# A recurrent scan on one core: 64-column tiles throughout, biases as weight rows, and both wrap pieces made on GpSimd

## The reference

```
x = x + conv3x3(gn(x)) + bias
x = x + scan(gn(x))
x = x + irfft2(low modes of rfft2(gn(x)), mixed over channels by w2)
x = x + irfft2(rfft2(gn(x)), mixed over channels by w3) + bias
```

```
x_  = [prev shifted down | prev | prev shifted up]       # along the rows, 96 features
i   = x_ @ weight_ih.T + bias_ih ;  h = cur @ weight_hh.T + bias_hh
r   = sigmoid(r_i + r_h) ; z = sigmoid(z_i + z_h) ; n = tanh(n_i + r * n_h)
new = n * z + cur * (1 - z)
```

## Time and profile before

| | |
|---|---|
| median of 3 runs | 661.55 us (659.97 to 664.05) |
| the profiled execution | 663.57 us, its span 661.8 us |
| PE busy | 595.9 us (90%) |
| DVE busy | 497.6 us (75%) |
| ACT busy | 456.2 us (69%) |
| POOL busy | 269.6 us (41%) |
| mean granted TensorE clock | 0.974 |
| the scan | about 132 to 377 us of the span |

### The profile page before, as it was taken

The page is one execution under the profiler, slowest core; times in us unless marked ns, Lnnn a source line. Parts: engine busy times, 40 slices in busy tenths (PEclk is TensorE's granted clock), DMA queues, the critical chain, the costliest instruction groups (busy, mean ns, idle before and its releaser), DMA issues.

```text
span 661.8 us, 19857 instructions
## 1 busy us (share of the span) xinstructions
PE 595.9 (90%) x6860; PEld 478.5 (72%) x6860; DVE 497.6 (75%) x1277; ACT 456.2 (69%) x932; POOL 269.6 (41%) x378
## 2 busy tenths in 40 slices
PE   4689888799999999999999999998878777799996
PEld 2223223478888888888888899997666666799996
DVE  6476685557777777777777768789889889867776
ACT  2345657877777777777777897776748997684442
POOL 6454546135555555554555430104485544202200
PEclk9799898979999999999999999999899998899999
DMA  6800000011111111111111210000316665203314
GB/s 236 316 1 0 1 0 9 0 31 35 36 34 34 35 36 34 34 36 34 35 34 36 62 79 1 1 1 1 129 34 219 201 212 164 96 1 128 128 78 176
DMA packets 31200, 45.63 MB, mean 69 GB/s; under 512 B 7088, under 2 KB 25520, under 8 KB 30272
## 3 DMA queue, kind: packets, MB, share of 16 engines
q1 hardware_dynamic: 30080, 44.98, 21.0%
q10 hardware_dynamic: 672, 0.15, 0.1%
q0 software_dynamic: 416, 0.07, 0.1%
HBM read 28.53 MB, written 8.39 MB: 56 GB/s over the span
## 4 chain that ended last, share of the span: by engine, by line
PE 71%; DVE 16%; issue 5%; ACT 5%; POOL 1%; DVEq 0%; ACTq 0%; POOLq 0%
PE psum L634 16%; PE psum L627 13%; PE psum L595 9%; PE psum L618 8%; DVE work L321 5%; PE psum L707 5%; PE psum L845 5%; PE psum L861 5%; PE psum L723 3%; PE psum L765 3%; ACT work L326 2%; DVE small L1161 2%; PE psum L834 2%; PE psum L691 2%; DVE spec L345 1%
## 5 line engine op out<-in xcount | busy, mean ns | idle before, releaser
L634 PE MATMUL psum<-spec,matrices 128*64 128x128 f32 x1512 | 111.7, 283 | 1.0 <-issue 1.0
L627 PE MATMUL psum<-spec,matrices 128*128 128x128 f32 x756 | 106.4, 277 | 2.3 <-DVE spec L1259 2.3
L486 POOL TENSOR_TENSOR spec<-spec 32x120 f32<-32x120 f32 x126 | 59.8, 474 | 119.0 <-DVE spec L1275 119.0
L595 PE MATMUL psum<-spec,matrices 128*64 128x512 f32 x384 | 94.2, 648 | 15.1 <-ACT spec L886 7.5
L765 PE MATMUL psum<-work 128*32 128x128 f32 x2368 | 77.4, 286 | 24.5 <-ACT work L326 22.2
L627 PEld LDWEIGHTS psum<-spec,matrices 128*128 128x128 f32 x756 | 95.2, 193 | 2.5 <-DVE spec L1259 2.5
L634 PEld LDWEIGHTS psum<-spec,matrices 128*64 128x64 f32 x1512 | 81.0, 138 | 16.5 <-issue 1.5
L765 PEld LDWEIGHTS psum<-work 128*32 128x32 f32 x2368 | 68.3, 115 | 33.4 <-issue 27.3
L595 PEld LDWEIGHTS psum<-spec,matrices 128*64 128x64 f32 x384 | 29.9, 148 | 72.8 <-issue 65.7
L321 DVE TENSOR_TENSOR work<-spec,psum 32x512 f32<-32x512 f32 x108 | 73.5, 680 | 9.1 <-PE psum L765 5.8
L461 POOL TENSOR_SCALAR spec<-image,small 32x960 f32<-32x960 f32 (+1 forms) x48 | 55.5, 1157 | 53.2 <-DVE small L1148 28.7
(11 more groups left out here) (140 smaller groups left out, 982.4 us busy)
## 6 DMA issues: line engine op xcount, KB each, us to landing
work<-w_dram SPq DMA_DIRECT2D x33, 512.0 KB, 3.4
spec<-work SPq DMA_DIRECT2D x252, 32.0 KB, 1.8
image<-x_dram SPq DMA_DIRECT2D x3, 2048.0 KB, 11.6
out_dram<-image SPq DMA_DIRECT2D x3, 2048.0 KB, 6.3
image<-x_dram SPq DMA_DIRECT2D x4, 512.0 KB, 5.9
work<-w_dram SPq DMA_DIRECT2D x1, 2048.0 KB, 7.6
out_dram<-image SPq DMA_DIRECT2D x4, 512.0 KB, 2.9
kept<-const_dram SPq DMA_DIRECT2D x1, 192.0 KB, 5.9
```

Source lines behind the costliest of these rows:

```text
L486: nc.gpsimd.tensor_tensor(lower_edge(h, parity), below(mix[h]), below(keep[h]), ALU.subtract).then_inc(lower_ready[h], 1)
L595: last_mm = mm(psum[o, n % 4, :], cv[:, kx, o], rows_[:, 8 * half:8 * half + 8, kx:kx + W], start=kx == 0, stop=kx == 2)
L627: mm(psum[:, 4 * h + g, 0:HB], sv[:, g, :], state[h], start=True, stop=False)
L634: last = mm(psum[o, 4 * h + g, 0:HB], sv[:, 3 + g, o], e, start=False, stop=True)
```

## The change

- **Tiles.** `from_state` issues two matmuls of 64 weight columns for each sum in place of one of 128. The h sum is no longer made by L618 from `columns` but by two 64-column matmuls from the edge buffers, whose current rows and ones it uses (weights of block 6). So all 14 matmuls of a half-step have 64 columns (6 from the state, 8 from the edges).
- **Order.** State part of r and n; wait for the edges; edges of r, of h, of n; state part of z; edges of z. VectorE waits for a new semaphore `h_sum`.
- **Biases.** VectorE spreads them in a zeroed 128 x 128 buffer `bias_z` (a memset and three small copies), TensorE turns them with eight small matmuls against the identity, and ScalarE writes them in two copies into the weight rows that the ones meet. This stands between the third and the fourth convolution group. ScalarE's activations have no bias any more, and pre1 is a plain product.
- **Wrap pieces.** GpSimd makes the lower one, waits for it, makes the upper one from `mix` and `keep`, waits for it, and then adds the state. ScalarE's copy is gone.
- **DMAs.** The edge buffers of the two halves lie side by side, so SP fetches a column for both halves in two DMAs of 256 columns, after z_sum of both halves. Only column 1 is fetched for each half apart.

```diff
         def edges_of(h, parity):
-            at_ = (2 * h + parity) * HB
+            at_ = (2 * parity + h) * HB
...
+            def current(w, parity):
+                for e, q in SIDES:
+                    sp.dma_start(e[q, parity * 2 * HB:(parity + 1) * 2 * HB],
+                                 columns[q, ds(w * (2 * HB), 2 * HB)]).then_inc(cur_in[parity], 16)
...
                     for h in range(2):
                         sp.wait_ge(z_sum[h], i * 2 + (k + 1))
-                        current(h, i * 2 + (k + 3), (k + 1) % 2)
+                    current(i * 2 + (k + 3), (k + 1) % 2)
...
                 nc.gpsimd.tensor_tensor(lower_edge(h, parity), below(mix[h]), below(keep[h]),
                                         ALU.subtract).then_inc(lower_ready[h], 1)
+                pool.wait_ge(lower_ready[h], w + 1)
+                nc.gpsimd.tensor_tensor(upper_edge(h, parity), above(mix[h]), above(keep[h]),
+                                        ALU.subtract).then_inc(sedge_ready[h], 1)
+                pool.wait_ge(sedge_ready[h], w + 1)
                 pool.wait_ge(state_ready[h], w + 1)
                 add_state(h, w)
...
+            pe.wait_ge(const_in, 32)
+            pe.wait_ge(bias_spread, 4)
+            for g in range(4):
+                for row in (C, 2 * C):
+                    last = mm(psum[row:row + C, 5, P * g:P * g + P], bias_z[:, C * g:C * g + C], cm["ident"],
+                              start=True, stop=True)
+            last.then_inc(bias_turned, 1)
             conv_group(NG - 1, False, True)
...
+            def from_state(h, w, g):
+                if g == 0:
+                    pe.wait_ge(state_ready[h], w)
+                for o in HALVES:
+                    mm(psum[o, 4 * h + g, 0:HB], sv[:, g, o], state[h], start=True, stop=False)
+
+            def from_edges(h, g, parity, starts=False):
+                for o, e in zip(HALVES, edges_of(h, parity)):
+                    last = mm(psum[o, 4 * h + g, 0:HB], sv[:, 3 + g, o], e, start=starts, stop=True)
+                return last
+
+            def half_step(h, w, parity, nth):
+                from_state(h, w, 0)
+                from_state(h, w, 2)
+                if nth is None:
+                    pe.wait_ge(cur_first[h], 32)
+                else:
+                    pe.wait_ge(cur_in[parity], nth * 32)
                 pe.wait_ge(sedge_ready[h], w)
                 pe.wait_ge(lower_ready[h], w)
+                from_edges(h, 0, parity).then_inc(r_sum[h], 1)
+                from_edges(h, 3, parity, True).then_inc(h_sum[h], 1)
+                from_edges(h, 2, parity).then_inc(n_sum[h], 1)
+                from_state(h, w, 1)
+                from_edges(h, 1, parity).then_inc(z_sum[h], 1)
...
+            for row, o in ((C, slice(P // 2, P)), (2 * C, slice(0, P // 2))):
+                a(sv[row:row + C, 3:7, o], turned[row:row + C, :, o], ACT.Copy).then_inc(bias_written, 1)
...
-            def state_edges(h, w, parity):
-                act.wait_ge(state_ready[h], w + 1)
-                s = state[h].rearrange("p (b h) -> p b h", h=H4)
-                up = edges_of(h, parity)[0].rearrange("p (b h) -> p b h", h=H4)
-                a(up[P - C:P, :, 1:H4], s[P - C:P, :, 0:H4 - 1], ACT.Copy).then_inc(sedge_ready[h], 1)
...
+            def scan_step(w):
+                for h in range(2):
+                    gates(h, w)
+                    candidate(h, w)
...
+            v.memset(bias_z, 0.0).then_inc(bias_spread, 1)
+            dve.wait_ge(bias_spread, 1)
+            v.tensor_copy(bias_z[:, 0:3 * C:C + 1], bias_s[:, 0:3]).then_inc(bias_spread, 1)
+            v.tensor_copy(bias_z[:, 3:3 + C + 2:C + 1], bias_s[:, 3:5]).then_inc(bias_spread, 1)
+            v.tensor_copy(bias_z[:, 3 * C + 5:3 * C + 6], bias_s[:, 5:6]).then_inc(bias_spread, 1)
...
             def new_state(h, w):
+                dve.wait_ge(h_sum[h], w)
                 dve.wait_ge(r_gate[h], w)
-                v.scalar_tensor_tensor(out=pre1[h], in0=psum[:, 4 * h + 3, 0:HB], scalar=bias_s[:, 5:6], in1=gr[h],
-                                       op0=ALU.add, op1=ALU.mult).then_inc(reset_done[h], 1)
+                v.tensor_tensor(pre1[h], gr[h], psum[:, 4 * h + 3, 0:HB], ALU.mult).then_inc(reset_done[h], 1)
```

More of the change, by code:

```diff
@@ L153, in edges_of @@
         def edges_of(h, parity):
-            at_ = (2 * h + parity) * HB
+            at_ = (2 * parity + h) * HB
             return upper_e[:, at_:at_ + HB], lower_e[:, at_:at_ + HB]
         gr, gz, gn, pre1, pre2, keep, mix = [[scan_buf() for _ in range(2)] for _ in range(7)]
+        bias_z = spec[:, off:off + 4 * C]
         columns = work[:, 0:B * ROWS]
@@ L198, in program @@
         columns_ready, last_columns = sem("columns_ready"), sem("last_columns")
-        bias_ready = sem("bias_ready")
-        cur_in = [[sem(f"cur_in{h}{parity}") for parity in range(2)] for h in range(2)]
+        bias_spread, bias_turned, bias_written = map(sem, ("bias_spread", "bias_turned", "bias_written"))
+        cur_first = [sem(f"cur_first{h}") for h in range(2)]
+        cur_in = [sem(f"cur_in{parity}") for parity in range(2)]
         state_ready = [sem(f"state_ready{h}") for h in range(2)]
         sedge_ready = [sem(f"sedge_ready{h}") for h in range(2)]
+        h_sum = [sem(f"h_sum{h}") for h in range(2)]
         lower_ready = [sem(f"lower_ready{h}") for h in range(2)]
@@ L386, in _, with first_current @@
             sp.dma_start(forward_m, const_d[:, sum(KEPT_COLS.values()):]).then_inc(const_in, 16)
[L388 to L392 removed]
+            SIDES = ((upper_e, slice(0, P // 2)), (lower_e, slice(P // 2, P)))
+            def first_current(h):
+                for e, q in SIDES:
+                    sp.dma_start(e[q, 2 * HB + h * HB:2 * HB + (h + 1) * HB],
+                                 columns[q, 2 * HB + h * HB:2 * HB + (h + 1) * HB]).then_inc(cur_first[h], 16)
+            def current(w, parity):
+                for e, q in SIDES:
+                    sp.dma_start(e[q, parity * 2 * HB:(parity + 1) * 2 * HB],
+                                 columns[q, ds(w * (2 * HB), 2 * HB)]).then_inc(cur_in[parity], 16)
             sp.wait_ge(pads_zeroed, 12)
             sp.wait_ge(columns_ready, B // 2)
[L396 to L397 removed]
+            first_current(0)
             sp.wait_ge(columns_ready, B)
             sp.wait_ge(last_columns, 1)
[L400 to L401 removed]
+            first_current(1)
+            current(2, 0)
             with sp.Fori(0, (W - 4) // 2) as i:
@@ L473, in lower_edge, with upper_edge, above @@
                 return edges_of(h, parity)[1].rearrange("p (b h) -> p b h", h=H4)[0:C, :, 0:H4 - 1]
+            def upper_edge(h, parity):
+                return edges_of(h, parity)[0].rearrange("p (b h) -> p b h", h=H4)[P - C:P, :, 1:H4]
+            def above(buf):
+                return buf.rearrange("p (b h) -> p b h", h=H4)[P - C:P, :, 0:H4 - 1]
             def below(buf):
@@ L493, in _ @@
                 nc.gpsimd.tensor_copy(lower_edge(h, 1), below(state[h])).then_inc(lower_ready[h], 1)
+                pool.wait_ge(lower_ready[h], 1)
+                nc.gpsimd.tensor_copy(upper_edge(h, 1), above(state[h])).then_inc(sedge_ready[h], 1)
+                pool.wait_ge(sedge_ready[h], 1)
                 add_state(h, 0)
@@ L613, in _ @@
             keep_warm(WARM_CONV_NORM, group_m)
-            def from_column(h, w):
-                mm(psum[:, 4 * h + 3, 0:HB], sv[:, 6, :], columns[:, ds(w * (2 * HB) + h * HB, HB)],
-                   start=True, stop=True)
-            def banks_free(h, w):
-                pe.wait_ge(reset_done[h], w - 1)
-            def from_state(h, w, parity, nth):
-                pe.wait_ge(state_ready[h], w)
-                for g in (0, 2, 1):
-                    mm(psum[:, 4 * h + g, 0:HB], sv[:, g, :], state[h], start=True, stop=False)
-                pe.wait_ge(cur_in[h][parity], nth * 32)
+            HALVES = [slice(i * (P // 2), (i + 1) * (P // 2)) for i in range(2)]
@@ L629, in from_state @@
                 pe.wait_ge(sedge_ready[h], w)
                 pe.wait_ge(lower_ready[h], w)
-                for g, s in ((0, r_sum), (2, n_sum), (1, z_sum)):
-                    for i, e in enumerate(edges_of(h, parity)):
-                        o = slice(i * (P // 2), (i + 1) * (P // 2))
-                        last = mm(psum[o, 4 * h + g, 0:HB], sv[:, 3 + g, o], e, start=False, stop=True)
-                    last.then_inc(s[h], 1)
+                from_edges(h, 0, parity).then_inc(r_sum[h], 1)
@@ L659, in _ @@
             with pe.Fori(0, (W - 4) // 4) as i:
                 for k in range(4):
-                    scan_step(i * 4 + (k + 2), k % 2, i * 2 + (1 + (k + 1) // 2))
-            scan_step(W - 2, 0, W // 2 - 1)
-            from_state(0, W - 1, 1, W // 2)
-            banks_free(1, W - 1)
-            from_column(1, W - 1)
-            from_state(1, W - 1, 1, W // 2)
+                    for h in range(2):
```

(6 more changed lines are left out.)

59 lines of the change are left out of this document (17 added, 42 removed).

## The result

The changed kernel takes 665.57 us (median; 663.60 to 667.22), the one before 662.72 us beside it on the same chip: a ratio of 1.0044 [1.0030, 1.0058], 2.9 us. The forecast was 672, slower by 1.6%. The profiled execution has a span of 664.1 us.

What follows compares the result with a forecast made beforehand. The prediction took TensorE at 1.89 us a half-step as the bound, the recurrence loop nearly as long. Its terms, 0 + 9.5 + 0.5 + 0 - 0.3 + 0.6 = +10.3 us on a median of 661.55, gave 672 us, range 657 to 689.

Steps and rivals of the forecast that it cites:

- likeliest case: Scan: half the mixes caught by GpSimd's add, half-step 1.92 to 2.05 us, 665 to 682 us; chance 0.46.
- border gain: TensorE in the scan: 0.35 us a half-step at two tile-width changes, 44 us by itself, but off the path.
- recurrence: Scan's loop through ScalarE, VectorE and GpSimd to TensorE: 3.78 us, 1.89 for a half-step, so 0 us.
- contention: VectorE's mix waiting for GpSimd's add in SBUF: half caught, mean 0.15 us a loop, +9.5 us, bounds 0 and +25.
- VectorE's loop border: VectorE idle 0.24 us once in six half-steps, mostly hidden afterwards: 0 to 2 us, taken as +0.5.
- Start -0.3: Start of the scan: ScalarE's 0.30 us copy ahead of its first gate goes, -0.3 us.
- End +0.6: End of the scan: last adds come 0.8 us later and ScalarE's staging waits for such an add, +0.6 us.
- bias rows: Bias work ahead of the last convolution group, inside 3.17 us of idle TensorE loads: 0 us, uncovered +3.
- Not caught: Scan: GpSimd's add never meets the mix; half-step 1.89 us, 662 us (657 to 667); chance 0.24.
- Fully coupled: Scan: every mix caught by GpSimd's add, delay feeding delay; half-step 2.09 us, 688 us; chance 0.13.
- The faster one: Scan: shorter recurrence, GpSimd's pieces at 0.40 us and no catch; half-step 1.80 us, 651 us; chance 0.13.
- rival (4): TensorE's idle time in the scan drops its clock to 1.2 GHz: +69 us, 731 us; chance 0.04.

Runs made afterwards that it cites:

- e7: The changed kernel with GpSimd's residual add cut to one of its 128 columns: 644.33 us, 0.9729 of the kernel before.
- e12: The changed kernel with GpSimd's add cut to one column and the state's part of z issued ahead of the wait for the edges: 641.62 us, 0.9670.
- e11: The changed kernel with GpSimd's add cut to one column and zero columns as bias operands of the three activations: 653.59 us, 0.9862.
- after: The changed kernel itself, against the kernel before: 665.57 us, 1.0044.
- e3: The changed kernel with the z gate written to PSUM, so mix and keep have only one operand in SBUF: 646.85 us, 0.9757.
- e1: The changed kernel with a column of zeros in SBUF as bias operand of its three activations: 676.91 us, 1.0222.
- e4: The changed kernel with the state's part of z issued ahead of the wait for the edges: 661.65 us, 0.9978.
- e2: The changed kernel with the upper piece made by ScalarE's copy of the new state again, not by GpSimd: 634.03 us, 0.9567.
- e8: The changed kernel with the upper piece on ScalarE, z's state part before the edge waits, VectorE's loop unrolled by 7: 630.07 us, 0.9516.
- e5: The changed kernel with the upper piece on ScalarE and a zero column as bias operand in its three activations: 643.05 us, 0.9703.
- e6: The kernel before the change with the bias operand left out of its three activations: 661.57 us, 0.9975.

## Why the prediction was right in its path and wrong in two terms

What happened is what its likeliest case says: the border gain is off the path, GpSimd's two pieces are on it, half of the mixes are caught. The size was off: 2.9 us for 10.3. Two terms of the sum failed, by more than the result itself and in opposite directions: the recurrence by 16 us and the contention by 11. That the time came out as near as it did, and T inside the 1.92 to 2.05 of the likeliest case, is luck.

**The recurrence, priced at 3.78 us for two half-steps ("Against 1.89 now: 0.00 x 126 = 0 us"), is 3.52.** The steps from the edge loads, predicted, and as e7 has them with no mix caught (loads at 299.60, the next of the same half at 303.10; the rows between are this kernel's timeline):

```profile
300.10 0.28 ACT L965 ACTIVATE spec<-psum 128x128 f32<-128x128 f32 x1 [0.46 <-PE psum L654]
...
300.98 0.28 ACT L967 ACTIVATE spec<-psum 128x128 f32<-128x128 f32 x1 [0.60 <-PE psum L654]
...
301.20 0.31 ACT L971 ACTIVATE spec<-spec 128x128 f32<-128x128 f32 x1
...
301.39 0.29 DVE L1288 SCALAR_TENSOR_TENSOR spec<-spec,work 128x128 f32<-128x128 f32 x1 [0.23 <-ACT spec L967]
301.60 0.28 DVE L1291 TENSOR_TENSOR spec<-spec 128x128 f32<-128x128 f32 x1
...
302.03 0.48 POOL L500 TENSOR_TENSOR spec<-spec 32x120 f32<-32x120 f32 x1 [0.55 <-DVE spec L1291]
...
302.59 0.44 POOL L503 TENSOR_TENSOR spec<-spec 32x120 f32<-32x120 f32 x1
...
303.10 0.66 PEld L654 LDWEIGHTS psum<-spec,matrices 128*64 128x64 f32 x12 [0.39 <-issue]
```

| step | predicted | e7 |
|---|---|---|
| second sigmoid | 1.36, lasting 0.37 | 1.38, lasting 0.28 |
| tanh | 1.75, lasting 0.40 | 1.60, lasting 0.31 |
| mix | 2.19 | 2.00 |
| lower piece | 2.62 | 2.43 |
| upper piece | 3.20, lasting 0.48 | 2.99, lasting 0.44 |
| next edge loads | 3.78 | 3.50 |

Up to the second sigmoid it is right within 0.02. The first 0.19 was lost between there and the mix: the prediction named the weight rows that replace the bias and changed the product L1264 for it (0.35 to 0.29), but left the three activations at their old durations, though the operand goes from them too. It also let tanh wait for the sigmoid's end; it starts 0.06 before. What holds the mix is then keep, which follows the second sigmoid, as the rows show and e12 against e7 bears out. The rest is small: the upper piece 0.04, the self-wait 0.08 for 0.10, and 0.07 for 0.10 from the piece to the load. In all (1.89 - 1.761) x 126 = 16 us to the good, of which the operand is 8.8 (e11); how the rest divides is read from the rows, not measured apart.

**The contention, priced at "mean 0.15 in each 3.78 loop" (+9.5 us), costs 21 us.** The share of mixes caught, one half, was right, and so was the single catch: 0.34 by the rows above, for a range of 0.20 to 0.40 taken. What failed is the other half. The sentence "the mix sometimes gets in first and the add waits instead" gave those steps a delay of zero. In the rows after, with this half's edge loads at 302.83 and e7's steps from there: pre1 at 1.06 for 0.88, because VectorE comes from the caught mix and the state behind it; tanh at 1.77 for 1.60; mix at 2.11 for 2.00, so 0.11 late; and the lower piece at 2.78 for 2.43, so 0.35 late, as it stands behind the lengthened add. The uncaught half is as late as the caught one, and a round of two periods costs 0.34 in either; T shows (1.927 - 1.761) x 2 = 0.33. Had the prediction taken its own mean for every loop, 0.30, it would have had 19 us here.

The Trainium skill (SBUF — State Buffer, section "SBUF: two separate sides") says of the shared port pair that the one that starts first has it whole. The trace agrees in both directions, the mix 0.63 where the add is first and the add 0.68 where the mix is. The prediction named both directions and priced only the one in which VectorE waits.

The recurrence and the contention together, -16 + 21 = +5, are what T of the two kernels shows, +3.7, but for 0.008 x 126 = 1 us: the prediction counted the period before as 1.89 and not 1.898.

**The other terms.** VectorE's loop border +0.5: nothing, as every sixth half-step is as long as the others of its half (1.58 or 2.27 between state operations). Start -0.3: measured -1.1, by the first state; no run says what the rest is. End +0.6: measured +0.1 (from the last state to the end). The bias rows are hidden as predicted, as far as that earlier start shows: three VectorE copies at 98 us of 0.14 to 0.45, and sixteen small loads at 99.03, ahead of the last convolution group. The merged DMAs show up in no wait of note, and the clock stays 0.99.

**The rivals.** Not caught (T 1.89, 662 us) happened nowhere as such; e3 and e7, where no mix is caught, run at 1.77 and 1.76. Fully coupled (2.09) is what e1 comes near: T 2.031 with both halves caught. The faster one, a shorter recurrence with no catch, was put at T 1.80 and "when the two pieces together are under 0.8": they are 0.92, and the loop is shorter for another reason, but its condition that the mix not be caught is what e3 brings about, 2.4% below the kernel before. The clock, rival (4), stayed at 0.99 with a stop of 0.28 or 0.42 in each half-step.

What stays open is what settles how many halves are caught. In "after" it is one of the two throughout, in e1 both, but for the mix behind VectorE's loop border (one in six), and in e4 one half with gaps; no run here moves the phase alone.

## What to carry to other kernels

When an operand is dropped from an instruction, reprice every instruction that loses it, and find another row of the same shape without it: here the term was worth 9 us and the sum did not have it. When two engines share something, price both outcomes: whichever gets in second is late, and the queue behind it on its own engine with it; one operand in PSUM took the mix out of the contention here (e3). And before work is moved to an engine that stands at 41%, ask what it will stand beside: the same edits with the upper piece left on ScalarE give 0.957 (e2), with z early and a longer unrolling 0.952 (e8), and with it on GpSimd 1.004.

## What the runs showed of the hardware

- A per-partition bias operand in SBUF costs a 128x128 activation 0.09 us: 0.37 for 0.28 (sigmoid from PSUM), 0.40 for 0.31 (tanh), in the kernel before, e1, e5 and e11 alike; without it in "after" and e6.
- Two activations one behind the other can overlap, by 0.06 (302.38 + 0.28 and 302.60, after) or 0.10 (e5, with the operand).
- A VectorE operation caught by a GpSimd one ends 0.14 or 0.15 after it (303.64 for 303.50; 301.94 for 301.80), in all 62 mixes and 61 states of "after". In e3 none of 126 mixes with a single SBUF operand is caught, while 22 states with two are.
- Even a GpSimd add of one column, 0.19 us alone, takes 0.30 when VectorE's mix has started 0.03 before it (299.68 and 299.71 in e7).
- GpSimd's product on 32 x 120 takes 0.48 as the lower piece, with partitions 0 to 31 as its output, and 0.44 as the upper one, with 96 to 127, by the medians of every kernel that has both. The last upper piece of the scan takes 1.31 in "after" (379.48), beside VectorE's copy for the next layer (379.02 to 380.49).
